# A hand-ordered adaLN transformer block on one core: norms and values change quarters, and two copies move to ScalarE

## The reference

```
h = layernorm(x) * (1 + ca) + sa
qkv = h @ Wqkv + bqkv                          # 16 heads of 8 channels
dist2 = |k|^2 + |q|^2 - 2 k.q                  # per head, 256 x 256
x = x + ga * ((exp(-sigma * dist2) @ v) @ Wproj + bproj)
h = layernorm(x) * (1 + cb) + sb
mask = the two largest of 8 router logits      # router: h @ w_router + b_router
x = x + gb * sum over experts e of mask[e] * (h @ We[e] + be[e])
```

## Time and profile before

| | |
|---|---|
| median of 3 runs | 234.09 us (230.92 to 234.24) |
| the profiled execution's own time | 233.86 us |
| its span in the trace | 232.1 us |
| busy: PE, DVE, ACT, POOL | 218.4, 177.7, 161.1, 140.3 us |
| share of PE in the chain that ended last | 81% |
| mean granted TensorE clock | 0.979 |

### The profile page before, as it was taken

How to read it: one execution, slowest core, us unless ns; L and a number is a source line. 1 busy time by engine, 2 the same in 40 slices (tenths; PEclk the granted TensorE clock), 3 DMA queues, 4 the chain that set the end, 5 groups by cost and what they waited for, 6 DMA issues and landing times.

```text
span 232.1 us, 6441 instructions
## 1 busy us (share of the span) xinstructions
PE 218.4 (94%) x2406; PEld 152.2 (66%) x2406; DVE 177.7 (77%) x620; ACT 161.1 (69%) x226; POOL 140.3 (60%) x204
## 2 busy tenths in 40 slices
PE   7879998999999999999999999999999999998980
PEld 6654454667676677676676766677766767665770
DVE  5797446686878787878878686978787886958785
ACT  3355787776887767687778787676878776786260
POOL 6415465636858484857577685848485765405465
PEclk9995899999999999999999999999999999999997
DMA  5455115231332333333323233323332321310001
GB/s 159 130 196 172 68 60 148 82 116 57 121 109 103 82 139 90 138 90 128 104 79 109 90 110 104 116 85 138 90 135 73 114 94 51 113 46 25 23 0 47
DMA packets 21265, 22.82 MB, mean 98 GB/s; under 512 B 2090, under 2 KB 19058, under 8 KB 21234
## 3 DMA queue, kind: packets, MB, share of 16 engines
q1 hardware_dynamic: 20906, 22.05, 30.2%
q10 hardware_dynamic: 328, 0.36, 0.5%
HBM read 6.65 MB, written 2.12 MB: 38 GB/s over the span
## 4 chain that ended last, share of the span: by engine, by line
PE 81%; DVE 5%; ACT 4%; POOL 4%; issue 2%; DMA 2%; SPq 1%; POOLq 0%; ACTq 0%; DVEq 0%
PE att_ps L888 25%; PE scores L871 11%; PE qkv_ps L897 7%; PE ffn_ps L991 6%; PE ffn_ps L992 5%; PE ffn_ps L993 5%; PE mid_ps L937 4%; PE mid_ps L951 3%; PE qkv_ps L906 3%; PE qkv_ps L916 3%; PE mid_ps L968 2%; DMA st<-norm_parts 2%; ACT probs L467 2%; PE qkv_ps L926 2%; PE scores L824 2%
## 5 line engine op out<-in xcount | busy, mean ns | idle before, releaser
L467 ACT ACTIVATE probs<-scores 128x1024 f32<-128x1024 f32 x128 | 125.3, 1020 | 32.8 <-PE scores L871 32.8
L888 PE MATMUL att_ps<-probs,vpad 128*32 128x256 f32 x1024 | 70.2, 393 | 0.0
L657 DVE SCALAR_TENSOR_TENSOR acc<-ffn_ps,mask,acc 128x128 f32<-128x128 f32 x218 | 61.3, 343 | 1.2 <-PE ffn_ps L993 1.2
L888 PEld LDWEIGHTS att_ps<-probs,vpad 128*32 128x32 f32 x1024 | 27.1, 111 | 20.3 <-issue 1.4
L348 POOL TENSOR_TENSOR ve<-stats,eps 128x2 f32<-128x2 f32 x32 | 6.2, 193 | 55.7 <-DVE stats L637 55.7
L871 PE MATMUL scores<-st 32*128 32x256 f32 x512 | 36.8, 333 | 3.0 <-ACT probs L467 2.0
L991 PE MATMUL ffn_ps<-we_hi,h_hi 128*128 128x256 f32 x110 | 36.9, 335 | 0.6 <-POOL h_lo L405 0.6
L386 POOL TENSOR_TENSOR sq<-qkf 128x512 f32<-128x512 f32 x15 | 19.0, 1264 | 21.1 <-DVE qkf L663 21.1
L871 PEld LDWEIGHTS scores<-st 32*128 32x128 f32 x512 | 22.9, 186 | 12.1 <-issue 3.8
L992 PE MATMUL ffn_ps<-we_hi,h_lo 128*128 128x256 f32 x110 | 30.7, 279 | 0.0
L993 PE MATMUL ffn_ps<-we_lo,h_hi 128*128 128x256 f32 x110 | 30.6, 278 | 0.0
(11 more groups left out here) (145 smaller groups left out, 348.1 us busy)
## 6 DMA issues: line engine op xcount, KB each, us to landing
st<-hl SPq DMA_DIRECT2D x48, 256.0 KB
rb_all<-rb_rows SPq DMA_DIRECT2D x16, 192.0 KB, 3.3
out_dram<-x_all SPq DMA_DIRECT2D x16, 128.0 KB, 3.0
x_all<-in_L_attn_x_dram SPq DMA_DIRECT2D x13, 128.0 KB, 3.3
st<-norm_parts SPq DMA_DIRECT2D x31, 32.0 KB
we_sb<-in_L_ffn_w_experts_dram SPq DMA_DIRECT2D x1, 512.0 KB, 6.3
w_mod_sb<-in_L_wmod_dram SPq DMA_DIRECT2D x1, 256.0 KB, 5.7
x_all<-in_L_attn_x_dram SPq DMA_DIRECT2D x1, 256.0 KB, 2.7
```

What stands on the lines that cost most here:

```text
L467: nc.scalar.activation(probs[:, g, 2 * half:2 * half + 2, :], scores[:, 2 * half:2 * half + 2, :], ACT.Exp, scale=two_sigma).then_inc((exp ...
L657: v.scalar_tensor_tensor(acc[:, q, t, :], y, m, acc[:, q, t, :], ALU.mult, ALU.add).then_inc(acc_step, 1)
L888: i = pe.matmul(att_ps[r * ROWS:(r + 1) * ROWS, 0:T], heads[:, g * ROWS:(g + 1) * ROWS], probs[:, g, r, t * T:(t + 1) * T], start=(g == 0 ...
```

## The change

On PE, in step k:

- `norms(k+1)` goes from the third quarter to the second, `values(k+1)` from the second to the third. `values` now waits for `norm_ok`, `norms` no longer waits for `v_ok`.
- `pv(k, 0)` and `pv(k, 1)` are cut into halves by token half. The second quarter keeps only the first half of group 0; the third gets the second half of group 0 and the first of group 1; the fourth the second half of group 1 and all of group 2.
- `qk_rows(k+1)` goes ahead of `turn_mask(k-2)`; in the tail `project(15)` goes ahead of `turn_mask(14)`.

On ACT: the two halves of `exp(k, 0)` now follow each other, `heads_out` comes ahead of `mask_rows`, and ACT takes over `high_parts` (for blocks 2 and up) and the copy `norm_hi` (for blocks 1 and up; it stands between `exp(k, 1)` and `exp(k, 2)`). On DVE both copies go away, `norm_rows` stands where `values` stood and the other way round. POOL and SP keep their lists.

```diff
@@ ScalarE
+            def high_parts(b):
+                act.wait_ge(qkf_ok, b + 1)
...
                 nc.scalar.copy(hl[:, 0:4:2, :], qkf[:, :, :]).then_inc(hi_ok, 1)
+
+            def norm_high(b):
+                act.wait_ge(n_ps, b + 1)
+                nc.scalar.copy(norm_hi[:, :], qkv_ps[0:NN, 0:T]).then_inc(nh_ok, 1)
@@ VectorE, step(k)
-                elif has(k + 1) and k > 0:
-                    high_parts(k + 1)
...
-                if has(k + 1) and k >= FILL:
-                    values(k + 1)
+                if has(k + 1) and k >= 0:
+                    norm_rows(k + 1)
...
+                    values(k + 1)
@@ TensorE, pv
+            def pv(b, g, halves=range(NT)):
+                if 0 in halves:
+                    pe.wait_ge(exp_a, G * b + g + 1)
+                    pe.wait_ge(exp_b, G * b + g + 1)
...
+                if NT - 1 in halves:
+                    i.then_inc(pv_done, 1)
@@ TensorE, values and norms
-                if b > FILL:
-                    pe.wait_ge(qkf_ok, b + 1)
-                elif b > 0:
+                if b > 0:
                     pe.wait_ge(norm_ok, b + 1)
...
                 pe.wait_ge(sq_ok, b + 1)
-                if b > FILL:
-                    pe.wait_ge(v_ok, b + 1)
@@ TensorE, tail
                 pv(b, 3)
+                project(b)
                 turn_mask(b - 1)
-                project(b)
```

More of the change, by code:

```diff
@@ L500, in step @@
                     heads_out(k - 1)
+                if has(k - 2):
+                    mask_rows(k - 2)
                 if k == -1:
-                    first_high_parts()
+                    high_parts(0)
                     preset()
@@ L508, in step @@
                     nc.scalar.copy(be_hi[:, :], be_sb[:, :]).then_inc(be_hi_ok, 1)
+                if has(k + 1) and k > 0:
+                    high_parts(k + 1)
                 if has(k - 2):
@@ L513, in step @@
                     exp(k, 1, 1)
+                if has(k + 1) and k >= 0:
+                    norm_high(k + 1)
                 if has(k):
@@ L754, in step @@
                     first_parts()
-                elif has(k + 1) and k > 0:
-                    high_parts(k + 1)
                 if has(k - 3):
                     experts(k - 3, 3)
-                if has(k + 1) and k < FILL:
-                    norm_rows(k + 1)
+                if k == -1:
+                    norm_rows(0)
                 if k == NB - 1:
@@ L874, in qk_scores @@
                             i.then_inc((qk_a, qk_b)[r // 2], 1)
[L876 to L879, removed]
[L880 to L885 removed]
+            def pv(b, g, halves=range(NT)):
+                if 0 in halves:
+                    pe.wait_ge(exp_a, G * b + g + 1)
+                    pe.wait_ge(exp_b, G * b + g + 1)
+                    if g == 0:
+                        pe.wait_ge(v_ok, b + 1)
+                        if b > 0:
+                            pe.wait_ge(o_ok, b)
+                        else:
+                            pe.wait_ge(wr_sb_ok, 1)
+                for t in halves:
                     for r in range(R):
@@ L1013, in step @@
                     pv(k - 1, 3)
+                if has(k + 1) and k > 0:
+                    qk_rows(k + 1)
                 if has(k - 2):
                     turn_mask(k - 2)
-                if has(k + 1) and k > 0:
-                    qk_rows(k + 1)
                 if has(k - 3):
@@ L1025, in step @@
                     qk_scores(k, 1)
-                    pv(k, 0)
-                if has(k + 1) and k < FILL:
+                    pv(k, 0, (0,))
+                if has(k + 1) and k >= 0:
                     norms(k + 1)
@@ L1036, in step @@
                     qk_scores(k, 2)
-                    pv(k, 1)
-                if has(k + 1):
-                    if k < FILL:
-                        values(k + 1)
-                    else:
-                        norms(k + 1)
+                    pv(k, 0, (1,))
+                    pv(k, 1, (0,))
+                if has(k + 1) and k >= 0:
+                    values(k + 1)
                 if has(k - 2):
```

21 lines of the change are left out of this document (6 added, 15 removed).

## The result

The changed kernel took 237.33 us (median of five, 236.68 to 239.06), the kernel before on the same chip 232.52 (median of five, 230.92 to 234.24; the forecast knew three of these). The ratio is 1.020, with an interval from 1.014 to 1.026. The forecast was 236.2 us with a range to 239.5, on the side that came: slower. The profiled execution is the slowest of the five, 239.06 us, with a span of 236.9.

A forecast was written before the change was run, and what follows sets the result against it. PE's own list was taken to bound the middle steps. Terms +1.95 + 0.5 - 0.3 - 0.3 + 0.5 = +2.35 us on the profiled 233.86 gave 236.2 us, range 232.6 to 239.5.

The forecast's parts named there:

- PE's list and the norms' wait, steps 2 to 14: Steps 2 to 14: dearer matmul neighbours on PE, +1.95 us, and PE waiting for the squares before norms, +0.5 us.
- steps 0 and 1: Ramp: step 0 gains from half a `pv` less, step 1 takes most back; -0.3 us, bounds -1.0 and +0.5.
- opening of step 15: Opening scores of step 15: the wait for the norms' DMA goes, -0.3 us, bounds 0 and -0.4.
- step 15 and tail: Tail: the mask's transposes and copy now follow `project`, delaying `expert_bias`; +0.5 us, bounds 0 and +0.8.
- standing directly behind narrow weights costs 0.18 us: Second and third quarter: `values` behind `pv` pays 0.18 us, and `project` behind the narrow `norms` goes on paying it.
- the rival that the list costs the same: PE's list: the 0.18 us may belong to `project` itself, so full steps add only 0.5; 234.3 us, chance 0.16.
- the 0.15 a step: PE's list, steps 2 to 14: net of 0.18 us more for `values` and 0.03 saved at the first expert matmul.
- I count nothing for it: Swap of `turn_mask` and `qk_rows` on PE: taken as free; at worst +0.33 us a step, +4.3 in all.
- The squares: Before the moved norms: squares shorten from 1.28 to 1.04 us once DVE's cast is gone; PE waits 0.03 to 0.04.
- lets the third scores go about 0.8 us earlier: Step 0 at half clock: half a `pv` less in the second quarter frees the third scores about 0.8 us earlier.
- the ramp's rival: Ramp: step 1 does not take back step 0's gain and later waits shrink, up to 1.5 us go; chance 0.11.
- the list's -0.4: PE's list, lower bound: if `project` behind `norms` costs only 0.37 us, -0.03 a step, -0.4 in all.

The follow-up runs named there:

- the filled pair: Kernel before and changed kernel, each with ten extra unused 128x128 matmuls where PE idled at the start and in step 0: 232.50 and 236.31 us.
- the filled one: Kernel before with ten extra unused matmuls on PE, three ahead of the first norms and seven in step 0: 232.50 us.
- the full step without the swap: Filled changed kernel with all of the mask's order put back and whole `pv` groups: 233.11 us, ratio 0.997; without the filling matmuls 234.26 us, ratio 1.002.
- the pair with a mean clock of 0.71 in both: Changed kernel run again unaltered, its profile set against the first one of the kernel before: 237.90 us, ratio 1.013.

## Why the prediction was right, and where it was not

By its own steps, with the filled pair as the measure:

| term | forecast | measured |
|---|---|---|
| PE's list and the norms' wait, steps 2 to 14 | +1.95 + 0.5 = +2.45 | +2.25: step 2 +0.52, steps 3 to 13 +1.29, step 14 +0.44 |
| steps 0 and 1 | -0.3 | +0.55: +0.45 and +0.10 |
| opening of step 15 | -0.3 | -0.28 against the plain kernel before, -1.19 against the filled one |
| step 15 and tail | +0.5 | +1.24 |

**The list: right size, wrong place, so the number is luck.** The step that failed is "standing directly behind narrow weights costs 0.18 us", read from `project` against `values`. Of the 0.18, `values` pays 0.10 behind `pv` (0.47 in place of 0.37), and `project` pays 0.09 less behind `norms` than it paid behind `pv` (0.46 in place of 0.55). So the place has a price, but it moves from one to the other, and the full step without the swap is 12.64 us. For these two quarters the rival that the list costs the same was right in its result, though not in its reason. What stood in for the 0.15 a step is the swap, for which I had written "I count nothing for it". I had also written that both orders change between narrow and full weights equally often in a step. That holds for the second and third quarter only. In the first, narrow `pv`, narrow mask, `qk_rows`, experts have one such change; narrow `pv`, `qk_rows`, narrow mask, experts have three. Those two more changes cost 0.11 us, 2.27 against 2.16. The Trainium skill, in "TensorEngine Tiling (Array Packing)", section Key Properties, says that a change of tiling mode drains TensorE. By that rule the second and third quarter are free and the first pays; the runs agree on both, and I should have counted the changes in all four quarters and not only where the big pieces moved. No run separates such a drain from another cause of the 0.11.

**The squares: right.** The cast and POOL's instruction exclude each other; with the cast on ACT all fifteen squares take 1.04 us. The Trainium skill, in "SBUF — State Buffer", section Who interferes with whom, has this rule, and the trace agrees: 1.28 with VectorE's cast issued first, 1.04 without. The wait at the norms was forecast as 0.04 us and is 0.46 - 0.445, some 0.02. The margin is as thin as forecast: with `qk_rows` behind the mask again, the norms came 0.62 us behind the half `pv`.

**The ramp: wrong sign.** The term said -0.3, with a bound of +0.5. What failed is that half a `pv` less in the second quarter of step 0 "lets the third scores go about 0.8 us earlier" and that part of this lives on: it was worked out at half clock, where the profile before had step 0. At full clock PE waits for `exp` there, and the half `pv` comes back whole in the last quarter: +0.45. In the pair with a mean clock of 0.71 in both, step 0 wins nothing either, and steps 0 and 1 lose 0.57 together. In the filled pair step 1 took +0.10, so the DMA wait of 0.74 us that went at its end was more than used up by the wait for the squares (0.90 in the profile after) and what follows it. In step 2 the bias stalls for 0.45 us.

**Step 15 and tail: too small.** The tail's mechanism was right: from `project` to the bias it was 0.64 us and is 1.28, where +0.5 was forecast. The same mechanism in step 15, where `mask_rows` now stands behind both halves of `exp` and behind `heads_out`, was not in the sum: +0.61, of which the old order of the mask gives back 0.43. I had read the tail as a list of its own, and step 15 as if it were a full step.

With -0.3 for the opening of step 15, the measured terms of the filled pair are 2.85 + 1.19 - 0.3 = 3.7 us, near the 3.8 between its medians and the 3.9 of the two profiles with equal heads. The forecast's 2.35 was 1.4 short, and all of it lies in steps 0 and 1 and at the end. Of the 4.8 us between the first two spans, the other 0.9 is where the half clock fell. Whether the same holds for the 4.8 between the first medians is not shown.

**The time forecast was nearer than the difference, by luck.** 236.2 is 1.1 us under the measured 237.33, although 4.8 us came where 2.35 was forecast: the 233.86 on which the sum stands lay 1.3 above the 232.52 of the five executions before. Two figures at the low end do not follow from the terms: the ramp's rival gives 234.3 + 0.3 - 1.5 = 233.1 where 232.9 stands, and the low end of the range comes to 232.7 only with the list's -0.4 added. Neither bears on the result.

## What to carry to other kernels

In a kernel bound by one engine's list, count the changes between narrow and full weights over the whole step before and after, not only where the large pieces moved; a full-width one put between two narrow groups adds two, here for 0.11 us. Read the first and last steps as lists of their own, because a copy that hides behind the matmuls of a full step stands bare where those matmuls are missing. And when the ramp of two profiles differs, first compare durations of matmuls that the change has not touched, and look for two profiles with the half clock in the same place: here 0.9 of the 4.8 us between the spans was only where it fell.

## What the runs showed of the hardware

- In the head of the span the clock column read 1.00 over 11 to 17 us in both first profiles, while identical matmuls took 1.07 us in one and 0.62 in the other. There the pace has to be read from durations.
- TensorE's half clock lay in a different part of the head or ramp from one execution to the next of one and the same program (in the changed kernel the first scores started at 18.08 and 15.54 us, and step 0 had a mean granted clock of 0.83 and 0.71). With ten filling matmuls the granted clock was 1.00 in steps 0 to 2, and the ratio of the kernel before was 0.994 (0.990 to 0.998) and 0.996 (0.992 to 1.000), so the gain is 0.4 to 0.6%, the second time not clear of nothing.
- A wait for a DMA was four times as long (1.19 and 0.28 us) where the last DMA's issue on SP's queue took 1.54 us in place of 0.64.
- The stretch from the first scores to the end was 1.29 and 1.24 us shorter in the profiles without that wait, and the medians on one chip did not differ: a difference of profiles of about 1 us is not yet a gain.
